# A cross-attention and expert kernel whose experts' second layer changes from fp32 matmuls to three fp32r passes over high and low parts

## What is computed

```python
xm = input[None] * jnp.moveaxis(mask, -1, 0)[..., None]
h = jnp.einsum('ebsd,edh->ebsh', xm, W1) + b1[:, None, None, :]
h = jax.nn.relu(h)
y = jnp.einsum('ebsh,ehd->ebsd', h, W2) + b2[:, None, None, :]
out = jnp.sum(y * jnp.moveaxis(scores, -1, 0)[..., None], axis=0)
...
x = x + _L0_xattn_ref(ctx_1024, _layernorm(x, axis=-1), ...)
x = x + _L0_ffn_ref(_layernorm(x, axis=-1), ...)
```

## Time and profile before

| | |
|---|---|
| median of 3 runs | 346.72 us (346.6 to 346.85) |
| profiled execution, its own time | 347.57 us |
| its span, first to last instruction | 345.8 us |
| mean granted TensorE clock | 0.999 of full |
| TensorE busy | 338.2 us, 98% |
| GpSimd busy | 253.9 us, 73% |
| VectorE, ScalarE busy | 274.1 us, 194.7 us |

### The profile page before, as it was taken

The page is one execution under the profiler, slowest core; times in us unless marked ns, Lnnn a source line. Parts: engine busy times, 40 slices in busy tenths (PEclk is TensorE's granted clock), DMA queues, the critical chain, the costliest instruction groups (busy, mean ns, idle before and its releaser), DMA issues.

```text
span 345.8 us, 6136 instructions
## 1 busy us (share of the span) xinstructions
PE 338.2 (98%) x2355; PEld 231.4 (67%) x2355; DVE 274.1 (79%) x430; ACT 194.7 (56%) x257; POOL 253.9 (73%) x163
## 2 busy tenths in 40 slices
PE   7899999999999999999999999999999999999996
PEld 7576666574747566575847475655694468999996
DVE  4889766887989899988899999999929898267433
ACT  2555678584858567584848584765713544135341
POOL 5629999999999999999999899989893771210000
PEclk9999999999999999999999999999999999999999
DMA  4630000000010000000000000000000010000000
GB/s 126 209 98 2 0 0 4 0 17 0 2 30 17 15 2 0 3 1 2 2 15 2 1 0 17 0 2 0 2 3 0 1 27 5 2 0 2 30 3 30
DMA packets 6713, 5.81 MB, mean 17 GB/s; under 512 B 743, under 2 KB 5789, under 8 KB 6685
## 3 DMA queue, kind: packets, MB, share of 16 engines
q1 hardware_dynamic: 6389, 5.29, 5.0%
q10 hardware_dynamic: 296, 0.13, 0.1%
HBM read 4.89 MB, written 0.52 MB: 16 GB/s over the span
## 4 chain that ended last, share of the span: by engine, by line
PE 95%; DVE 2%; ACT 1%; issue 0%; POOL 0%; DVEq 0%; POOLq 0%
PE xo L415 23%; PE sc L395 20%; PE mx L617 8%; PE sc L401 6%; PE sc L321 6%; PE sc L322 5%; PE sc L323 5%; PE mx L352 3%; PE xo L352 3%; PE mx L504 2%; PE xo L504 2%; PE sc L436 2%; PE xo L424 2%; PE mx L322 1%; PE mx L321 1%; PE mx L323 1%
## 5 line engine op out<-in xcount | busy, mean ns | idle before, releaser
L1142 POOL TENSOR_TENSOR psum_acc<-psum_acc,probs 111x1024 f32<-111x1024 f32 x63 | 158.8, 2521 | 9.3 <-DVE psum_acc L864 1.9
L686 ACT ACTIVATE probs<-sc 111x1024 f32<-111x1024 f32 x96 | 98.2, 1026 | 18.7 <-PE sc L401 10.5
L415 PE MATMUL xo<-probs,v_sb 111*64 111x512 f32 x384 | 88.2, 596 | 0.0
L395 PE MATMUL sc<-q_pair,k_pair 64*111 64x512 f32 x576 | 85.5, 401 | 0.8 <-ACT v_sb L676 0.4
L395 PEld LDWEIGHTS sc<-q_pair,k_pair 64*111 64x111 f32 x576 | 44.3, 170 | 29.2 <-issue 12.2
L875 DVE RECIPROCAL recips<-recips 128x128 f32<-128x128 f32 x64 | 55.6, 913 | 0.0
L415 PEld LDWEIGHTS xo<-probs,v_sb 111*64 111x64 f32 x384 | 26.2, 137 | 42.3 <-issue 38.7
L841 DVE TENSOR_REDUCE part_max<-mx 128x2 f32<-128x888 f32 x32 | 34.7, 1084 | 16.2 <-PE mx L352 15.0
L1142 POOL TENSOR_TENSOR psum_acc<-probs 111x1024 f32<-111x1024 f32 x16 | 38.4, 2401 | 10.2 <-ACT probs L686 10.2
L401 PE MATMUL sc<-max_row,ones_r 64*111 64x512 f32 x192 | 38.0, 390 | 0.0
L777 ACT ACTIVATE probs<-sc,cols 128x512 f32<-128x512 f32 x32 | 21.5, 687 | 28.3 <-PE sc L323 28.0
(11 more groups left out here) (179 smaller groups left out, 525.1 us busy)
## 6 DMA issues: line engine op xcount, KB each, us to landing
w_raw<-in_L_ffn_W SPq DMA_DIRECT2D x8, 128.0 KB, 2.4
x_tok<-in_x SPq DMA_DIRECT2D x2, 256.0 KB, 3.0
wv_raw<-in_L_xattn_Wkv SPq DMA_DIRECT2D x4, 128.0 KB, 3.0
wout_sb<-in_L_xattn_Wout SPq DMA_DIRECT2D x1, 512.0 KB
wqk_raw<-in_L_xattn_Wq SPq DMA_DIRECT2D x7, 64.0 KB, 2.0
wqk_raw<-in_L_xattn_Wkv SPq DMA_DIRECT2D x7, 64.0 KB, 2.0
out<-x_tok SPq DMA_DIRECT2D x1, 256.0 KB, 2.0
out<-x_tok SPq DMA_DIRECT2D x2, 128.0 KB, 1.7
```

Source lines behind the costliest of these rows:

```text
L395: pe.matmul(sc[0:KP, kt % 2, h, :], k_pair[r, s % QKB, k_part, at], q_pair[r, s % QKB, q_part, :], start=(k_part + q_part == 0), stop=False)
L415: mm = pe.matmul(o_ps[h * HD:(h + 1) * HD, :], v_sb[0:KP, s // 2 % 2, kt, at:at + HD], probs[0:KP, e % RING, h, :], start=(kt == 0), stop= ...
L686: act.activation(probs[0:KP, e % RING, :, :], sc[0:KP, kt % 2, :, :], ACT.Exp).then_inc(exp_done, 1)
L1142: pool.tensor_tensor(psum_acc[0:KP, s % 2, :, :], first, probs[0:KP, e % RING, :, :], ALU.add) \
```

## The change

The second layer takes the form of the first. relu's output is split as well as w2, and `expert_out` makes three fp32r passes for each plain fp32 matmul:

```diff
+RR = 4
+LAG = 2
-W1_AT = {2: 0, 3: 1, 9: 2, 11: 3}
+W1_AT = {2: (0,), 3: (1,), 8: (2, 3), 9: (4,), 10: (5,), 11: (6,), 12: (7,)}
+W2_AT = {12: (0,), 13: (1, 2), 14: (3, 4), 15: (5, 6), 16: (7,)}
...
-                        mm = pe.matmul(y_ps(g, t)[:, t * P:(t + 1) * P],
-                                       relu_ring[:, (g * HC + c) % FR, t * P:(t + 1) * P],
-                                       w2_sb[:, e * HC + c, :], start=(c == 0), stop=(c == HC - 1))
+                        n = (g * HC + c) % FR
+                        pe.matmul(y_ps(g, t)[:, at], relu_hi_ring[:, n, at], w2_hi(e)[:, c, :],
+                                  start=(c == 0), stop=False)
+                        pe.matmul(y_ps(g, t)[:, at], relu_hi_ring[:, n, at], w2_lo(e)[:, c, :],
+                                  start=False, stop=False)
+                        mm = pe.matmul(y_ps(g, t)[:, at], relu_lo_ring[:, n, at], w2_hi(e)[:, c, :],
+                                       start=False, stop=(c == HC - 1))
...
+                if g == 7:
+                    turn_x2(1)
-                if g >= 1:
-                    expert_out(g - 1)
+                if g >= LAG:
+                    expert_out(g - LAG)
...
+            def w1_high(e):
+                act.wait_ge(w1_loaded[e % 2], 16 * (e // 2 + 1))
+                act.copy(w1_hi[:, e, :], w1_from(e)).then_inc(w1_hi_ready, 1)
+
+            def w2_high(e):
+                act.wait_ge(tail_loaded, 16 * 4)
+                act.wait_ge(k_lo_done, 2 * (STEPS - WB + e // 2 + 1))
+                act.copy(w2_hi(e), w2_raw[:, e * HC:(e + 1) * HC, :]).then_inc(w2_hi_ready, 1)
...
             def relu(n):
                 act.wait_ge(hid_ready, n + 1)
+                if n >= RR:
+                    act.wait_ge(relu_hi_done, n - RR + 1)
+                    act.wait_ge(relu_lo_done, n - RR + 1)
+                act.activation(relu_ring[:, n % RR, :], hid_ps[:, n % 4, :], ACT.Relu,
+                               bias=cols[:, n % (E * HC):n % (E * HC) + 1]).then_inc(relu_done, 1)
+
+            def relu_high(n):
+                act.wait_ge(relu_done, n + 1)
                 if n >= FR:
                     act.wait_ge(y_ready, (n - FR) // HC + 1)
+                act.copy(relu_hi_ring[:, n % FR, :], relu_ring[:, n % RR, :]).then_inc(relu_hi_done, 1)
...
+            def w2_low(e):
+                pool.wait_ge(w2_hi_ready, e + 1)
+                raw = w2_raw[:, e * HC:(e + 1) * HC, :]
+                pool.tensor_tensor(w2_lo(e), raw, w2_hi(e).bitcast(F32), ALU.subtract).then_inc(w2_split, 1)
+
+            def relu_low(n):
+                pool.wait_ge(relu_hi_done, n + 1)
+                if n >= FR:
+                    pool.wait_ge(y_ready, (n - FR) // HC + 1)
+                pool.tensor_tensor(relu_lo_ring[:, n % FR, :], relu_ring[:, n % RR, :],
+                                   relu_hi_ring[:, n % FR, :].bitcast(F32), ALU.subtract).then_inc(relu_lo_done, 1)
...
                 if g == 3:
                     x1_and_moments(1, x1_ps[1])
+                    norm_x1(1)
                 if g == 4:
-                    norm_x1(1)
+                    split_x2(1)
                 if g == 5:
-                    split_x2(1)
+                    gate_start(1)
                 if g == 6:
-                    gate_start(1)
                     gate_end(1)
...
+            for g in range(B * E):
+                for c in range(HC):
+                    relu_low(g * HC + c)
+                if g == 0:
+                    for e in W2_AT[STEPS]:
+                        w2_low(e)
+                if g == 3:
+                    normalise(STEPS - 1)
+                if g == 5:
+                    rstd_x1(1)
```

More of the change, by code:

```diff
@@ L135, in xattn_moe @@
         w1_lo = sb("w1_lo", [P, E, HID], F32R)
-        w2_sb = sb("w2_sb", [P, E * HC, D])
         wg_sb = sb("wg_sb", [P, E])
@@ L305, in _ @@
                     load_v(2 + s // 4)
-                if s - 1 in W1_AT and W1_AT[s - 1] + 2 < E:
-                    load_w1(W1_AT[s - 1] + 2)
-            for e in (6, 7):
+                if s in (3, 4):
+                    load_w1(s - 1)
+            for e in range(4, E):
                 load_w1(e)
@@ L761, in _ @@
                     copy_sum(s - 1)
+                for e in W1_AT.get(s + 1, ()):
+                    w1_high(e)
+                for e in W2_AT.get(s + 1, ()):
+                    w2_high(e)
             def gate_exp_of(b):
@@ L1164, in _ @@
                     split_v(2 + s // 7)
-                if s in W1_AT:
-                    split_w1(W1_AT[s])
+                for e in W1_AT.get(s, ()):
+                    w1_low(e)
+                for e in W2_AT.get(s, ()):
+                    w2_low(e)
                 gather(s, 5)
@@ L1173, in _, with rstd_x1 @@
             normalise(STEPS - 3)
[L1174 to L1186 removed]
+            def rstd_x1(b):
                 pool.wait_ge(var_ready, 2 * B + b + 1)
```

89 lines of the change are left out of this document (54 added, 35 removed).

## The result

The kernel after takes 375.04 us (median of 6, 374.38 to 375.68) against 346.79 us for the kernel before in the same runs: a ratio of 1.0801 [1.0785, 1.0817]. Direction and main term were right, but the time is 4 us above the range of 360.5 to 371. The profiled execution took 374.38 us with a span of 372.6, 26.8 us more than before.

What follows compares the result with a forecast made beforehand. TensorE, busy for 338.2 of 345.8 us, was taken as the bound. Terms 14.2 + 0.4 + 0.6 + 1.5 + 1.3 + 0.5 = +18.5 us on the 346.72 median gave 365.2 us, range 360.5 to 371.

Steps and rivals of the forecast that it cites:

- Direction: Whole kernel: slower than before, chance 0.93.
- main term: Experts' output layer on TensorE: load-bound fp32r passes at 0.111 us each, +14.2 us over 16 rounds.
- More passes: Experts' output layer: 24 fp32r passes of 0.111 us, 2.67 us a round in place of 1.78, +14.2 us over all.
- ScalarE's casts and GpSimd's splits in the steps: Attention steps: added casts and subtractions fit into idle time, 0; casts at worst 0.1 us in each of four steps.
- turn_x2(0): Last step, before the experts: fourth norm on VectorE held for one w2 subtraction on GpSimd, +0.4 us.
- First expert_out: First expert's output layer: TensorE waits for GpSimd's first two low parts, +0.6 us.
- First gate: Batch 0's gate on VectorE: held by gapless GpSimd work, score at about 292 to 295, +1.5 us, bounds 0 and 3.
- x1 of batch 1: Ahead of turn_x2(1): VectorE's norm held by two GpSimd low parts, +1.3 us, bounds 0 and 3.
- Second gate: Batch 1's gate: its 3.4 us grow to some 7, against 6.9 us available, +0.5 us, bounds 0 and 2.
- The rival with 375 us: Gates and x1's norm: GpSimd and VectorE hold each other for every instruction, +28.5 us in all; chance 9%.

Runs made afterwards that it cites:

- the kernel with gaps: Against the kernel after: each GpSimd low part of relu waits for the one ahead of it, opening 0.14 us between two; 376.93 us (367.92 to 392.59).
- the first fp16 version: Against the kernel after: high and low parts of relu and w2 in fp16, low parts on VectorE with the first two early; 347.59 us, ratio 1.0022.

## Why the prediction was wrong, step by step

- *More passes, +14.2:* right. 24 passes in 2.63 us, against 2.67 said. Reading the load's rate off the logits gave the size. The 222-column passes did not help to choose, since 222 columns at the streaming rate of the earlier trace rows take 0.10 us as well; the logits did. The Trainium skill gives 81 ns for 128 columns ("TensorE: Matmul & The Clock Gate", "Back-to-back issue gap"), an estimate of +2.6 by that page; the measured distance with 4-byte operands is 111 ns, with 2-byte ones 56.
- *ScalarE's casts and GpSimd's splits in the steps, 0:* right within the half microsecond named; the attention steps end 0.5 earlier.
- *turn_x2(0), +0.4:* nothing measured. The fourth norm was held by the w2 subtraction, but turn_x2(0) starts at 274.01 against 274.53 before, early by the same 0.5 as its neighbours.
- *First expert_out, +0.6:* 0.9 measured, by the mechanism named.
- *First gate, +1.5, bounds 0 to 3:* **this step failed**; 4.7 measured. It took "one or two for each of its 1.3 us", from norms and a comparison in the rows, and counted from the first comparison. Three things went against it. The comparison in the rows had been held one for one, and one for one alone gives a wait of 3.4 us, as on 111 partitions. g_prob, ahead of the first comparison, was held by the whole stream, which made the other 1.2 us; no row showed that. The shapes differ, 111x1024 for the gathers in the earlier trace rows and 128x512 for relu's low parts, but low parts of 128x512 let norms and comparisons in all the same. And TensorE was there at 291.5, not at 292 to 293, while the score came at 296.0, where 292 to 295 was said.
- *x1 of batch 1, +1.3:* 2.3 measured, inside its bounds; the mechanism was right, the term too small: three low parts held the norms, not two.
- *Second gate, +0.5:* right, for the reason named: GpSimd has gaps there, and two of its comparisons took 1.3 us each, not all.
- *The clock:* **missing from the sum**, +4.6. Idle time of TensorE was priced at its own length. Nothing in the profile before showed the further price, because TensorE has no long wait in its experts; its clock of 0.999 was a sign that TensorE had not been left idle there, not that it could be.

The rival with 375 us has the right total by luck, from the wrong terms: it gave the first gate 6 us, the second 4, and the clock nothing. Of its idea, that hold is what costs, more was true than the 9% I gave: with low parts of 111 partitions each comparison of the first gate waited for at least one of GpSimd's instructions. The Trainium skill ("SBUF — State Buffer", "SBUF: two separate sides") says that VectorE, with two SBUF inputs, and GpSimd share a port pair under an exclusive lock that is held for a whole instruction. The traces agree for most of VectorE's instructions here, 1.3 us of hold for each; g_prob's 12.08 us beside ten GpSimd instructions is more than one whole instruction, and no run shows why.

## What to carry to other kernels

Price a pass by the side that is slower, operand bytes included: three fp32r passes are dearer than the two records of a plain fp32 matmul, three fp16 passes are cheaper. Before a stream goes onto GpSimd, look for a chain of small two-input instructions on VectorE beside it. As long as the stream has no gap, count one of GpSimd's instructions for each of the chain's, and know that a single one may be stopped for the whole length, as g_prob was on 128 partitions. And a wait of some microseconds on TensorE costs more than itself when the clock falls behind it, so take the wait away, or at least fill it.

## What the runs showed of the chip that I had not expected

- A gapless GpSimd stream of tensor-tensor instructions on 128 partitions held one VectorE tensor-tensor instruction of 128x32, g_prob, for 10.6 us (a normalise and eight subtractions) and 12.08 us (ten instructions). On 111 partitions the same stream, 9.86 us against 9.88, let g_prob in and then one instruction after each of its own. Other VectorE instructions got in one for one on 128 partitions too (comparisons at 335.94, norms at 318.04 in the kernel after), so what decides is open.
- Gaps of 0.14 us between the instructions ended g_prob's hold after 2.73 us and let one to three VectorE instructions in each time.
- In or just behind TensorE waits of 2.15 to 8.5 us the granted clock fell to half, which cost 1.4 and 3.2 us in the kernel after; it did not behind waits of 2.17 and 1.08 us in the profiled execution of the kernel with gaps, nor behind one of 1.87 us in the first fp16 version, and kept at work over the wait, TensorE stayed at 1.00.
- fp32r passes of 128 columns are 0.111 us apart and fp16 passes 0.056, at 2.4 GHz both.
